# Search units of the second head group moved into the Q, K, V projection stage

## The chip, the cores and the metric

The kernel is one program on one core of a Trainium2 chip. The time is the device time of one execution in microseconds; an execution is compared as the median of several runs of the same program.

## The reference, cut to what matters

Four layers follow one another on a sequence of 1024 tokens with 512 features, each with a residual and a layer normalisation behind it: a selective scan, a gated feed-forward layer, causal attention, and a feed-forward layer with 4-bit weights. The change touches the attention alone:

```python
q, k, v = (proj(wq), proj(wk), proj(wv))          # 32 heads of 16
q = _apply_rope(q, sin, cos)
k = _apply_rope(k, sin, cos)
scores = jnp.einsum('bnth,bnsh->bnts', q, k) * (1.0 / math.sqrt(h))
scores = jnp.where(causal, scores, -jnp.inf)
attn = jax.nn.softmax(scores, axis=-1)
out = jnp.einsum('bnts,bnsh->bnth', attn, v)
```

## The kernel before

PE is TensorE, DVE is VectorE, ACT is ScalarE, POOL is GpSimd, SP is the engine that issues the DMAs. The eight PSUM banks are the array `ps`; `arena` is one large SBUF array in which the buffers are views. All waits between engines are written out by hand as semaphores.

**Attention in head groups.** The 32 heads are worked on in 8 groups of 4 (`g` = 0 to 7), and each group in two halves of 512 query tokens (`half`). The softmax needs the largest score of every query row before the exponentials. So the scores are made twice: a **search** makes them with tokens on the partitions and DVE takes the row maximum (`reduce_max`, L1277); later the **keys** step makes them transposed (L705), with the negated maximum riding along as an extra row of the query operand, ACT takes the exponential (L954), POOL cuts the causal corner (L1054), and **values** multiplies by V (L721).

A **search unit** (`max_units`) is one query tile of 128 tokens against up to 512 keys for one head, or for two heads where two fit in a PSUM bank (L657); on the diagonal two small matmuls add the causal mask (L661). A group has 40 units: tile 0 and tile 1 have 2 each, tiles 2 and 3 have 4 each, tiles 4 and 5 have 6 each, tiles 6 and 7 have 8 each.

**The ring.** Every unit is written to a PSUM bank of a ring and may be written only after DVE has read the unit that was there before (`ring_slot`). In the projection stage the ring has two banks, in the attention it has three:

```python
elif n >= EARLY + RING:
    pe.wait_ge(ring_read, n - RING + 1)
elif n >= 2:
    pe.wait_ge(ring_read, n - 1)
```

**From maximum to key row.** When the units of a half are reduced, DVE negates the maxima (`negate`, L1296, L1298), PE turns them into rows (`turn_maxima`, L692), DVE copies the rows out (L1304), SP puts them with four small DMAs into the query operand (L411), and the first keys step of that group and half waits for these DMAs (`m_rows`).

**The Q, K, V projection stage.** For each of the eight token tiles `t`, PE makes the projections Q, K and V (`project`, L573, 12 matmuls each; `w` = 0, 1, 2), and behind the Q and the K projection it turns the tile before with 16 transposes (`turn_stack`, L634). DVE applies the rotary tables after Q and after K (`rope`, L1266 to L1268) and copies the turned keys (`keep_keys`, L1272). ACT and POOL split the result into two halves of the precision (L924, L1031, L1035). Search units of group 0 for tiles 0 to 5 (24 units, `EARLY_UNITS`) are already made here, those of tile `t - 2` in the iteration `t`, in up to three **places**, one behind each projection, two units per place:

```python
for n in early_units(t, w):
    pe.wait_ge(k_kept, t - 1)
    search(0, *EARLY_UNITS[n], n)
```

DVE reads the units of place 0 between the two `rope` calls, and those of the places 1 and 2 after the second `rope` and `keep_keys`:

```python
rope(0, t)
for n in early_units(t, 0):
    maxima(*EARLY_UNITS[n], n)
rope(1, t)
if t:
    keep_keys(t - 1)
for n in early_units(t, 1) + early_units(t, 2):
    maxima(*EARLY_UNITS[n], n)
```

**The order of the attention.** `attention_order` writes one list (`ORDER`) of all remaining units, negations, turns, keys and values steps, and all engines follow it. The "side" list (searches, negations, turns) and the "main" list (keys and values) are merged by a small model of the engines: at each point it takes what could start first. Early units are left out of the side list, so with fewer of them the whole merge comes out differently. The searches run about one group ahead of the keys.

Of the kernel before, what the change touches and what calls it, by code (L numbers as in the profile page):

```python
# [9 lines left out]
TT = T // P  # L10
# [12 lines left out]
GH = 4  # L23
# [34 lines left out]
def build(nc, x_fm, a_log, d_skip, xw, dtw, wg0, wu0, wd0, wq, wk, wv, wo,  # L58
          w1_q, w1_s, w1_z, ident, fold, mask, cos, sin, shifts, out):
    f32, f16, bf16, i32, u8 = mybir.dt.float32, mybir.dt.float16, mybir.dt.bfloat16, mybir.dt.int32, mybir.dt.uint8  # L60
    ALU = mybir.AluOpType
# [5 lines left out]
    with ctx:  # L67
# [83 lines left out]
        o_tok = view(32, TT * D, f32).rearrange("p (i d) -> p i d", i=TT)  # L151
        o_raw = view(188, T, f32)
        m_row = view(192, T, f16)
        m_a = view(199, TT * GH, f32).rearrange("p (i a) -> p i a", i=TT)
        m_b = view(199.25, 4 * GH, f32).rearrange("p (i a) -> p i a", i=4)
        m_neg = [view(199.5 + h / 8, 4 * GH, f16).rearrange("p (i a) -> p i a", i=4) for h in range(2)]
        r_den = view(199.75, 4 * GH, f32).rearrange("p (i a) -> p i a", i=4)
        oh = view(96, DC * T, f16).rearrange("p (c t) -> p c t", c=DC)
# [37 lines left out]
            return units  # L196
        SEARCH = [max_units(half) for half in range(2)]
        EARLY_TILES = TT - 2
        EARLY_UNITS = [(half, k) for half in range(2) for k, unit in enumerate(SEARCH[half]) if unit[0] < EARLY_TILES]
        EARLY = len(EARLY_UNITS)  # L200

        def early_units(t, place):

            units = [n for n, (half, k) in enumerate(EARLY_UNITS) if SEARCH[half][k][0] == t - 2]
            return units[2 * place:2 * place + 2]

        def maxima_slot(half, k):

            i, key, _, heads = SEARCH[half][k]
            dst = m_b[:, i - 4, :] if key else m_a[:, i, :]  # L210
            r, b = heads[0]
            return dst[:, b:GH:2] if len(heads) == 2 else dst[:, 2 * r + b:2 * r + b + 1]

# [21 lines left out]
        def attention_order():  # L235
# [9 lines left out]
            for g in range(NG):  # L245
                for half in range(2):
                    for k in range(len(SEARCH[half])):
                        if k == TURN_AFTER:
                            side, turn = side + turn, []
                        if g or (half, k) not in EARLY_UNITS:  # L250
                            side.append(("search", g, half, k))
                    side.append(("negate", g, half))
                    if g == 0 and half == 0:
                        side.append(("turn", g, half))
                    else:
                        turn = [("turn", g, half)]
# [64 lines left out]
        def ring_bank(n):  # L321
            return n % 2 if n < EARLY else (n - EARLY) % RING
# [119 lines left out]
        def _(pe):  # L442
# [222 lines left out]
            for t in range(1, TT):  # L665

                for w, signal in ((0, q_proj), (1, k_proj), (2, v_proj)):
                    if w:
                        pe.wait_ge(roped, 2 * t - 2 + w)
                    elif t >= 2:  # L670
                        pe.wait_ge(v_kept, t - 1)
                    project(w, xh, xl, t, qkv_bank(t, w), signal)
                    if w == 0 and t >= 2:
                        pe.wait_ge(k_kept, t - 1)
                    if w == 1:
                        pe.wait_ge(q_kept, t)
                    if w < 2:
                        turn_stack(w, t - 1)
                    for n in early_units(t, w):
                        pe.wait_ge(k_kept, t - 1)  # L680
                        search(0, *EARLY_UNITS[n], n)
            pe.wait_ge(k_kept, TT - 1)
            turn_stack(0, TT - 1)
            pe.wait_ge(q_kept, TT)
# [391 lines left out]
        def _(dve):  # L1076
# [194 lines left out]
                dve.wait_ge(k_turned, t + 1)  # L1271
                nc.vector.tensor_copy(k_st[:, :, ds(t * P, P)], banks(6, 2).bitcast(f16).rearrange("p (r t) -> p r t", r=NP)).then_inc(k_kept, 1)  # L1272

            def maxima(half, k, n):
                _, _, w, heads = SEARCH[half][k]
                dve.wait_ge(ring_full, n + 1)
                nc.vector.reduce_max(maxima_slot(half, k), ps[:, ring_bank(n), 0:len(heads) * w].rearrange("p (a w) -> p a w", a=len(heads)),  # L1277
                                     AX).then_inc(ring_read, 1)

            for t in range(TT):  # L1280
# [11 lines left out]
            def negate(g, half):  # L1292
                last = RING_AT.get(("search", g, half, len(SEARCH[half]) - 1), EARLY - 1)
                dve.wait_ge(ring_read, last + 1)
                if half:
                    nc.vector.tensor_tensor(m_a[:, 4:TT, :], m_a[:, 4:TT, :], m_b[:], ALU.max).then_inc(m_joined, 1)  # L1296
                    dve.wait_ge(m_joined, g + 1)
                nc.vector.tensor_scalar(m_neg[half][:], m_a[:, 4 * half:4 * half + 4, :], -1.0, None, ALU.mult).then_inc(m_negated, 1)  # L1298

            def keep_rows(g, half, n):  # L1300
                dve.wait_ge(ring_full, n + 1)
# [26 lines left out]

            for kind, g, half, *at in ORDER:
                if kind == "search":  # L1330
                    maxima(half, *at, RING_AT[kind, g, half, *at])
                elif kind == "negate":
                    negate(g, half)
                elif kind == "turn":
                    keep_rows(g, half, RING_AT[kind, g, half])
                elif kind == "out":
                    if g == NG - 1 and half == 1:
                        dve.wait_ge(ld_shift, 16)
                        nibbles(0, 0, 1)
                        dve.wait_ge(st_full, EXP_TO[-1])  # L1340
                        unscaled(0)
                        nibbles(1, 1, 1)
                    divide(g, half, RING_AT[kind, g, half])
# [105 lines left out]
```

## Time and profile before

| what | value |
|---|---|
| median of 3 runs | 942.63 us (940.75 to 944.0) |
| profiled execution, its own time | 939.31 us |
| span of its trace | 937.6 us |
| PE busy | 822.3 us (88%) |
| DVE busy | 670.3 us (71%) |
| ACT busy | 398.6 us (43%) |
| POOL busy | 297.3 us (32%) |
| projection stage, main part | 411.7 to 488.0 us |
| attention | 493.6 to about 723 us |

Busy time is the share in which an engine executes instructions; it is an average over stages with different limits, so the stages are read one by one. The span begins at the first instruction and ends at the last; the 1.7 us to the execution's own time lie around it. The first search reduction starts at 428.0 us and the last at 698.9 us.

### The profile page before, as it was taken

The numbers are of one execution on the slowest core, as the hardware profiler recorded it, in microseconds if no ns is written. First come the engines' busy times: TensorE is split into PE (matmuls) and PEld (weight loads), VectorE is DVE, ScalarE is ACT, GpSimd is POOL, SyncE is SP. The second block draws the span as 40 slices with busy tenths as digits, with TensorE's granted clock in tenths as the row PEclk, the third lists the DMA queues.
The fourth block names the chain that finished last, engine by engine and source line by source line (L and its number), as shares of the span: only waits on it lengthen the run. The fifth ranks groups of instructions, "written<-read, shape, count | busy, mean of one in ns | idle before, by whom it ended". The sixth has DMA issues, their size and how long they took to land.

```text
span 937.6 us, 19520 instructions
## 1 busy us (share of the span) xinstructions
PE 822.3 (88%) x8096; PEld 386.3 (41%) x8096; DVE 670.3 (71%) x932; ACT 398.6 (43%) x455; POOL 297.3 (32%) x211
## 2 busy tenths in 40 slices
PE   5556877776799999999998999999996999999997
PEld 1323333332544444445553334444431544444443
DVE  2899999997755334454567899999984878886344
ACT  3623646443253331144342667666675433333100
POOL 0356798988201001035441111122213223222000
PEclk9577899989799999999996899999999999999999
DMA  6700000001620000000000000000003203430011
GB/s 231 309 2 1 3 3 2 3 3 35 211 91 18 0 0 1 1 1 1 1 1 1 2 1 2 2 2 2 2 2 120 99 2 111 142 129 0 1 40 50
DMA packets 20222, 38.23 MB, mean 41 GB/s; under 512 B 6801, under 2 KB 10641, under 8 KB 20146
## 3 DMA queue, kind: packets, MB, share of 16 engines
q1 hardware_dynamic: 20146, 37.12, 11.4%
q8 instruction: 59, 0.97, 0.4%
q14 instruction: 17, 0.14, 0.0%
HBM read 34.89 MB, written 2.16 MB: 40 GB/s over the span
## 4 chain that ended last, share of the span: by engine, by line
PE 62%; DVE 11%; POOL 2%; ACT 2%; issue 1%; SPq 1%; DMA 1%; DVEq 0%; POOLq 0%; ACTq 0%
PE ps L770 12%; PE ps L595 10%; PE ps L573 8%; PE ps L797 6%; DVE arena L1277 6%; PE ps L721 5%; PE ps L619 5%; PE ps L657 5%; PE ps L705 3%; POOL arena L1007 2%; PE ps L634 2%; PE ps L661 1%; PE ps L730 1%; PE ps L462 1%; PE ps L542 1%
## 5 line engine op out<-in xcount | busy, mean ns | idle before, releaser
L1277 DVE TENSOR_REDUCE arena<-ps 128x1 f32<-128x512 f32 (+3 forms) x320 | 183.7, 629 | 20.7 <-PE ps L661 14.7
L1007 POOL TENSOR_TENSOR arena<-arena 128x1024 f32<-128x1024 f32 x64 | 157.0, 2476 | 72.9 <-DVE arena L1133 72.6
L954 ACT ACTIVATE arena<-ps 128x1024 f32<-128x1024 f32 (+2 forms) x160 | 144.1, 941 | 77.9 <-PE ps L705 77.7
L1133 DVE TENSOR_TENSOR_SCAN arena<-arena,ps 128x1024 f32<-128x1024 f32 x64 | 142.9, 2272 | 6.2 <-ACT arena L853 3.8
L770 PE MATMUL ps<-arena 128*128 128x512 f16 x528 | 114.3, 379 | 1.6 <-DVE arena L1212 1.6
L853 ACT ACTIVATE arena<-arena,negA 128x1024 f32<-128x1024 f32 x64 | 73.2, 1148 | 85.6 <-DVE arena L1133 83.4
L1054 POOL TENSOR_SCALAR_AFFINE_SELECT arena<-arena 128x512 f32<-128x512 f32 x64 | 42.5, 664 | 185.5 <-ACT arena L954 185.5
L492 PE MATMUL ps<-arena 64*128 64x64 f16 x3072 | 63.1, 200 | 43.0 <-DVE arena L1133 39.0
L595 PE MATMUL ps<-arena 128*128 128x512 f16 x448 | 98.6, 383 | 1.6 <-DVE arena L1212 1.6
L657 PE MATMUL ps<-arena 64*128 64x512 f16 (+3 forms) x384 | 97.6, 342 | 0.7 <-DVE arena L1277 0.5
L492 PEld LDWEIGHTS ps<-arena 64*128 64x128 f16 x3072 | 55.3, 101 | 102.3 <-DVE arena L1133 83.6
L462 PE MATMUL ps<-arena,ident_sb 64*64 64x512 f32 x512 | 78.3, 687 | 15.4 <-DVE arena L1142 12.3
L573 PE MATMUL ps<-arena 128*128 128x512 f16 x384 | 86.9, 379 | 3.0 <-DVE arena L1212 1.6
L721 PE MATMUL ps<-arena 128*32 128x512 f32 (+3 forms) x768 | 83.8, 509 | 1.9 <-POOL arena L1054 1.9
L705 PE MATMUL ps<-arena 64*128 64x512 f16 (+3 forms) x384 | 77.5, 338 | 4.3 <-DMA arena<-arena 2.3
L770 PEld LDWEIGHTS ps<-arena 128*128 128x128 f16 x528 | 51.6, 98 | 63.6 <-DVE arena L1212 1.8
L595 PEld LDWEIGHTS ps<-arena 128*128 (+1 forms) x448 | 44.2, 99 | 55.4 <-issue 2.1
L657 PEld LDWEIGHTS ps<-arena 64*128 64x128 f16 x384 | 29.2, 94 | 82.1 <-DVE arena L1277 69.8
L797 PE MATMUL ps<-arena 128*128 128x512 f16 x264 | 57.1, 379 | 0.0
L573 PEld LDWEIGHTS ps<-arena 128*128 128x128 f16 x384 | 36.4, 98 | 45.0 <-DVE arena L1186 1.8
L661 PE MATMUL ps<-mask_b,picks_b 64*128 64x128 bf16 x512 | 52.4, 219 | 0.0
L619 PE MATMUL ps<-arena 128*128 128x512 f16 x224 | 49.3, 379 | 0.0
(121 smaller groups left out, 940.9 us busy)
## 6 DMA issues: line engine op xcount, KB each, us to landing
arena<-in_w_q_dram SPq DMA_DIRECT2D x11, 768.0 KB, 4.2
arena<-c_rows SPq DMA_DIRECT2D x16, 512.0 KB, 9.7
arena<-in_w_s_dram SPq DMA_DIRECT2D x11, 384.0 KB, 4.5
arena<-in_x_fm_dram SPq DMA_DIRECT2D x4, 512.0 KB, 5.4
out_dram<-arena SPq DMA_DIRECT2D x8, 256.0 KB, 2.0
arena<-in_wg_dram SPq DMA_DIRECT2D x1, 1792.0 KB, 9.5
arena<-in_wu_dram SPq DMA_DIRECT2D x1, 1792.0 KB, 7.4
arena<-in_wd_dram SPq DMA_DIRECT2D x1, 1792.0 KB, 12.3
```

The source lines that it names most:

```text
L492: last = nc.tensor.matmul(ps[:, 2 * (i % 2) + r, q * SUB:(q + 1) * SUB], dtx_tok[c % 2][rows, s, q, :], diag[n][rows, e, q, :], start=(k = ...
L573: last = nc.tensor.matmul(banks(bank, 1), part[:, c, ds(t * P, P)], wsp[:, w, s, c, :], start=(c == 0 and part is src_h and s == 0), stop= ...
L595: last = nc.tensor.matmul(banks(bank + h, 1), w[:, c, ds(m * P, P)], part[:, c, h * HALF:(h + 1) * HALF], start=(c == 0 and part is xh), s ...
L657: last = nc.tensor.matmul(dst, q_st[rows, 2 * g + r, i * P:(i + 1) * P], k_st[rows, 2 * g + r, key:key + w], start=True, stop=not diag)
L705: last = nc.tensor.matmul(ps[:, 3 + 2 * (e % 2) + b, at * (hi - lo):(at + 1) * (hi - lo)], k_st[rows, 2 * g + r, j * P:(j + 1) * P], q_st[ ...
L721: last = nc.tensor.matmul(ps[32 * a:32 * a + 32, 7, lo - HALF * half:HALF], v_ring[g % 2][:, j, a, :], p_t[n % 4][:, a, 0:hi - lo], start= ...
L770: last = nc.tensor.matmul(banks(bank + h, 1), gu[u][:, s, w * DC + c, :], part[:, c, h * HALF:(h + 1) * HALF], start=(c == 0 and s == 0 an ...
L797: last = nc.tensor.matmul(banks(u, 1), part[:, m, ds(t * P, P)], wd1[:, s, m, :], start=(m == 0 and part is h1h and s == 0), stop=(m == M1 ...
L954: nc.scalar.activation(dst, src, ACT.Exp, scale=float(HD) ** -0.5).then_inc(exp_done, 1)
L1007: nc.gpsimd.tensor_tensor(hC[i % 4][:], hst[i % 3][:], c_all[:, n, :], ALU.mult).then_inc(hc_done, 1)
L1133: nc.vector.tensor_tensor_scan(hst[i % 3][:], dA[i % 3][:], banks(2 * (i % 2), 2), 0.0, ALU.mult, ALU.add).then_inc(scan_done, 1)
L1277: nc.vector.reduce_max(maxima_slot(half, k), ps[:, ring_bank(n), 0:len(heads) * w].rearrange("p (a w) -> p a w", a=len(heads)), AX).then_i ...
```

## The change

The search units of groups 0 and 1 for the tiles 0 to 5 are now both made in the projection stage: 48 units in place of 24, four per place in place of two, group 0 and group 1 alternating. The buffers for the maxima (`m_a`, `m_b`) are doubled, one set per parity of the group. The ring in the projection stage keeps its two banks. The side list of the attention order loses the 24 units of group 1.

```diff
@@ -151,8 +151,8 @@
-        m_a = view(199, TT * GH, f32).rearrange("p (i a) -> p i a", i=TT)
-        m_b = view(199.25, 4 * GH, f32).rearrange("p (i a) -> p i a", i=4)
+        m_a = [view(199 + u / 8, TT * GH, f32).rearrange("p (i a) -> p i a", i=TT) for u in range(2)]
+        m_b = [view(199.25 + u / 16, 4 * GH, f32).rearrange("p (i a) -> p i a", i=4) for u in range(2)]
@@ -196,18 +196,19 @@
-        EARLY_UNITS = [(half, k) for half in range(2) for k, unit in enumerate(SEARCH[half]) if unit[0] < EARLY_TILES]
+        EARLY_GROUPS = 2
+        EARLY_UNITS = [(g, half, k) for half in range(2) for k, unit in enumerate(SEARCH[half]) if unit[0] < EARLY_TILES for g in range(EARLY_GROUPS)]
...
-            units = [n for n, (half, k) in enumerate(EARLY_UNITS) if SEARCH[half][k][0] == t - 2]
-            return units[2 * place:2 * place + 2]
+            units = [n for n, (_, half, k) in enumerate(EARLY_UNITS) if SEARCH[half][k][0] == t - 2]
+            return units[2 * EARLY_GROUPS * place:2 * EARLY_GROUPS * (place + 1)]
@@ -247,7 +248,7 @@
-                        if g or (half, k) not in EARLY_UNITS:
+                        if (g, half, k) not in EARLY_UNITS:
@@ -678,7 +679,7 @@
-                        search(0, *EARLY_UNITS[n], n)
+                        search(*EARLY_UNITS[n], n)
@@ -1293,9 +1294,9 @@
-                    nc.vector.tensor_tensor(m_a[:, 4:TT, :], m_a[:, 4:TT, :], m_b[:], ALU.max).then_inc(m_joined, 1)
+                    nc.vector.tensor_tensor(m_a[g % 2][:, 4:TT, :], m_a[g % 2][:, 4:TT, :], m_b[g % 2][:], ALU.max).then_inc(m_joined, 1)
```

The remaining lines of the diff pass the group's number through `maxima_slot` and `maxima`. Since one line is added, lines of the changed kernel have a number one higher (L657 is L658 there).

On PE in the projection stage, iteration t = 5, from the transposes behind the K projection to the V projection (place 1; L634 are the transposes, L657 and L661 a search unit, L573 a projection), before:

```order
L634 MATMUL ps<-ident_h,arena 128x128 x15
L657 MATMUL ps<-arena 128x512 [waits ring_read,k_kept]
L661 MATMUL ps<-mask_b,picks_b 128x128 x2
L657 MATMUL ps<-arena 128x512 [waits ring_read,k_kept]
L661 MATMUL ps<-mask_b,picks_b 128x128 x2
L573 MATMUL ps<-arena 128x512 [waits roped]
```

and in the changed kernel:

```order
L635 MATMUL ps<-ident_h,arena 128x128 x15
L658 MATMUL ps<-arena 128x512 [waits ring_read,k_kept]
L662 MATMUL ps<-mask_b,picks_b 128x128 x2
L658 MATMUL ps<-arena 128x512 [waits ring_read,k_kept]
L662 MATMUL ps<-mask_b,picks_b 128x128 x2
L658 MATMUL ps<-arena 128x512 [waits ring_read,k_kept]
L662 MATMUL ps<-mask_b,picks_b 128x128 x2
L658 MATMUL ps<-arena 128x512 [waits ring_read,k_kept]
L662 MATMUL ps<-mask_b,picks_b 128x128 x2
L574 MATMUL ps<-arena 128x512 [waits roped]
```

Two units more stand ahead of the V projection, and each unit waits for the reading of the unit two before it.

On DVE in the same stretch, from the second `rope` of t = 5 (L1266 to L1268) over `keep_keys` (L1272) to the reductions (L1277), before:

```order
L1266 TENSOR_TENSOR arena<-ps,cos_sb 128x512 [waits stack_low,k_proj]
L1267 TENSOR_TENSOR arena<-ps,sin_sb 128x32x8
L1268 TENSOR_TENSOR arena<-ps,sin_sb 128x32x8
L1272 COPY arena<-ps 128x16x128 [waits k_turned]
L1277 TENSOR_REDUCE arena<-ps 128x1 [waits ring_full] x2
```

and in the changed kernel:

```order
L1267 TENSOR_TENSOR arena<-ps,cos_sb 128x512 [waits stack_low,k_proj]
L1268 TENSOR_TENSOR arena<-ps,sin_sb 128x32x8
L1269 TENSOR_TENSOR arena<-ps,sin_sb 128x32x8
L1273 COPY arena<-ps 128x16x128 [waits k_turned]
L1278 TENSOR_REDUCE arena<-ps 128x1 [waits ring_full] x4
```

The reductions still stand behind `rope` and `keep_keys`, and there are four of them.

On DVE at the start of the attention, from the last searches of group 0 (L1277) over the negation (L1296, L1298) and the copy of the rows (L1304), before:

```order
L1277 TENSOR_REDUCE arena<-ps 128x1 [waits ring_full] x16
L1296 TENSOR_TENSOR arena<-arena 128x16 [waits ring_read]
L1298 TENSOR_SCALAR arena<-arena 128x16 [waits m_joined]
L1277 TENSOR_REDUCE arena<-ps 128x2 [waits ring_full] x2
L1304 COPY arena<-ps 4x512 [waits ring_full]
L1277 TENSOR_REDUCE arena<-ps 128x2 [waits ring_full] x2
L1277 TENSOR_REDUCE arena<-ps 128x1 [waits ring_full] x8
```

and in the changed kernel:

```order
L1278 TENSOR_REDUCE arena<-ps 128x1 [waits ring_full] x16
L1297 TENSOR_TENSOR arena<-arena 128x16 [waits ring_read]
L1299 TENSOR_SCALAR arena<-arena 128x16 [waits m_joined]
L1305 COPY arena<-ps 4x512 [waits ring_full]
L1299 TENSOR_SCALAR arena<-arena 128x16 [waits ring_read]
L1305 COPY arena<-ps 4x512 [waits m_rows0,ring_full]
L1278 TENSOR_REDUCE arena<-ps 128x1 [waits ring_full] x13
```

The rows of group 0, half 1 and of group 1, half 0 now follow each other directly, and the search units of group 1 for the tiles 0 to 5 are gone from here.

## Rows read from the trace of the kernel before

**Rows 1.** Busy time by stretch: start and end, length, engines busy, PEclk.

```profile
411.70:488.00 76.30, 76.30 (x569) 41.59 (x570) 41.24 (x78) 35.13 (x32) 37.99 (x32) 1.00 0.01 1
493.64:525.00 31.36, 29.08 (x203) 11.00 (x204) 23.50 (x46) 12.42 (x14) 2.54 (x4) 0.67 0.01 1
525.00:552.16 27.16, 26.55 (x276) 11.02 (x273) 25.07 (x50) 18.77 (x22) 5.63 (x9) 1.00 0.01 2
660.80:687.96 27.16, 26.56 (x276) 11.02 (x273) 25.06 (x50) 18.77 (x22) 5.63 (x9) 1.00 0.01 2
687.96:698.30 10.34, 10.34 (x103) 3.63 (x98) 9.75 (x17) 7.24 (x9) 2.54 (x4) 1.00 0.00 0
```

The five busy times are those of PE, PEld (weight loads), DVE, ACT and POOL; behind them stand the granted clock of PE, the share of the DMA engines and GB/s.

**Rows 2.** Chain of waits, 440 to 492 us, shares by line.

```profile
by line: PE ps L573 69.1%; PE ps L634 19.4%; PE ps L657 6.0%; ACT arena L915 3.6%; PE ps L661 2.2%; issue 0.1%
```

**Rows 3.** Timeline of t = 5: start, length, engine, line, operation, [idle before].

```profile
458.59 0.40 PE L657 MATMUL ps<-arena 64*128 64x512 f16 x2
459.03 2.76 PE L573 MATMUL ps<-arena 128*128 128x512 f16 x12
459.12 1.29 DVE L1277 TENSOR_REDUCE arena<-ps 128x1 f32<-128x512 f32 x2
462.62 0.40 PE L657 MATMUL ps<-arena 64*128 64x512 f16 x2
463.06 5.35 PE L573 MATMUL ps<-arena 128*128 128x512 f16 x24
463.10 1.21 DVE L1272 COPY arena<-ps 128x2048 f16<-128x2048 f16 x1
464.23 1.28 DVE L1277 TENSOR_REDUCE arena<-ps 128x1 f32<-128x512 f32 x2
```

**Rows 4.** Timeline, reductions and projections at the places of other iterations.

```profile
427.96 0.76 DVE L1277 TENSOR_REDUCE arena<-ps 128x2 f32<-128x256 f32 x2
448.52 1.02 DVE L1277 TENSOR_REDUCE arena<-ps 128x1 f32<-128x384 f32 x2
452.41 5.35 PE L573 MATMUL ps<-arena 128*128 128x512 f16 x24
453.63 1.01 DVE L1277 TENSOR_REDUCE arena<-ps 128x1 f32<-128x384 f32 x2
476.71 0.76 DVE L1277 TENSOR_REDUCE arena<-ps 128x2 f32<-128x256 f32 x2 [0.67 <-PE ps L661]
476.73 2.76 PE L573 MATMUL ps<-arena 128*128 128x512 f16 x12
487.90 1.29 DVE L1277 TENSOR_REDUCE arena<-ps 128x2 f32<-128x512 f32 x2 [0.78 <-PE ps L661]
```

**Rows 5.** Timeline of the attention: the ring runs full; below, one reduction alone.

```profile
508.19 3.75 DVE L1277 TENSOR_REDUCE arena<-ps 128x2 f32<-128x512 f32 x7
508.93 0.09 PEld L657 LDWEIGHTS ps<-arena 64*128 64x128 f16 x1 [0.47 <-DVE arena L1277]
509.53 0.09 PEld L657 LDWEIGHTS ps<-arena 64*128 64x128 f16 x1 [0.33 <-DVE arena L1277]
...
592.43 0.69 DVE L1277 TENSOR_REDUCE arena<-ps 128x2 f32<-128x512 f32 x1
```

**Rows 6.** Timeline at the end of the attention, where no search is left.

```profile
704.50 0.39 PE L705 MATMUL ps<-arena 64*128 64x512 f16 x2 [1.12 <-DMA arena<-arena]
704.99 2.86 ACT L954 ACTIVATE arena<-ps 128x1024 f32<-128x1024 f32 x3 [1.69 <-PE ps L705]
710.45 7.89 ACT L954 ACTIVATE arena<-ps 128x1024 f32<-128x1024 f32 x9 [0.28 <-PE ps L705]
```

**Rows 7.** Busy time by stretch, where the clock of PE falls or holds.

```profile
180.00:192.00 12.00, 9.44 (x292) 4.79 (x284) 12.00 (x7) 5.74 (x6) 11.33 (x6) 1.00 0.02 4
488.00:494.00 6.00, 2.44 (x39) 2.01 (x38) 2.50 (x4) 1.86 (x1) 1.57 (x3) 1.00 0.00 0
494.00:504.00 10.00, 9.41 (x48) 3.12 (x46) 8.43 (x15) 4.41 (x5) 1.27 (x2) 0.51 0.01 0
```

More of the change, by code:

```diff
@@ L198, in build, with maxima_slot @@
         EARLY_TILES = TT - 2
-        EARLY_UNITS = [(half, k) for half in range(2) for k, unit in enumerate(SEARCH[half]) if unit[0] < EARLY_TILES]
+        EARLY_GROUPS = 2
+        EARLY_UNITS = [(g, half, k) for half in range(2) for k, unit in enumerate(SEARCH[half]) if unit[0] < EARLY_TILES for g in range(EARLY_GROUPS)]
         EARLY = len(EARLY_UNITS)
         def early_units(t, place):
-            units = [n for n, (half, k) in enumerate(EARLY_UNITS) if SEARCH[half][k][0] == t - 2]
-            return units[2 * place:2 * place + 2]
-        def maxima_slot(half, k):
+            units = [n for n, (_, half, k) in enumerate(EARLY_UNITS) if SEARCH[half][k][0] == t - 2]
+            return units[2 * EARLY_GROUPS * place:2 * EARLY_GROUPS * (place + 1)]
+        def maxima_slot(g, half, k):
             i, key, _, heads = SEARCH[half][k]
-            dst = m_b[:, i - 4, :] if key else m_a[:, i, :]
+            dst = m_b[g % 2][:, i - 4, :] if key else m_a[g % 2][:, i, :]
             r, b = heads[0]
@@ L1272, in keep_keys, with maxima @@
                 nc.vector.tensor_copy(k_st[:, :, ds(t * P, P)], banks(6, 2).bitcast(f16).rearrange("p (r t) -> p r t", r=NP)).then_inc(k_kept, 1)
-            def maxima(half, k, n):
+            def maxima(g, half, k, n):
                 _, _, w, heads = SEARCH[half][k]
                 dve.wait_ge(ring_full, n + 1)
-                nc.vector.reduce_max(maxima_slot(half, k), ps[:, ring_bank(n), 0:len(heads) * w].rearrange("p (a w) -> p a w", a=len(heads)),
+                nc.vector.reduce_max(maxima_slot(g, half, k), ps[:, ring_bank(n), 0:len(heads) * w].rearrange("p (a w) -> p a w", a=len(heads)),
                                      AX).then_inc(ring_read, 1)
@@ L1295, in negate @@
                 if half:
-                    nc.vector.tensor_tensor(m_a[:, 4:TT, :], m_a[:, 4:TT, :], m_b[:], ALU.max).then_inc(m_joined, 1)
+                    nc.vector.tensor_tensor(m_a[g % 2][:, 4:TT, :], m_a[g % 2][:, 4:TT, :], m_b[g % 2][:], ALU.max).then_inc(m_joined, 1)
                     dve.wait_ge(m_joined, g + 1)
-                nc.vector.tensor_scalar(m_neg[half][:], m_a[:, 4 * half:4 * half + 4, :], -1.0, None, ALU.mult).then_inc(m_negated, 1)
+                nc.vector.tensor_scalar(m_neg[half][:], m_a[g % 2][:, 4 * half:4 * half + 4, :], -1.0, None, ALU.mult).then_inc(m_negated, 1)
             def keep_rows(g, half, n):
@@ L1330, in _ @@
                 if kind == "search":
-                    maxima(half, *at, RING_AT[kind, g, half, *at])
+                    maxima(g, half, *at, RING_AT[kind, g, half, *at])
                 elif kind == "negate":
```

## The prediction

> **What bounds the kernel now.** I read the busy time by stretch first. In the projection stage PE is busy in all of its 76.30 us, DVE in 41.24 [rows 1]: to the reader this says that DVE has 35 us to spare, and that whatever delays PE here delays the kernel. The chain of waits agrees: from 440 to 492 us nearly all of it is PE, projections, transposes and searches [rows 2], with no wait for DVE in it. In the attention six equal periods of 27.16 us follow each other, one per head group; the first and the last of them are shown, with PE busy 26.55, DVE 25.07 and ACT 18.77 us [rows 1]. There both PE and DVE are nearly full. So the change takes reductions from where DVE is short and puts them where it has time. The question is whether PE can hand them over there without standing still. For that I read the timeline of one iteration [rows 3], then the same places of the others [rows 4].
>
> **Part 1, two more units at each place.** The units stand in the order t = 2 and 3: place 0 alone; t = 4 and 5: places 0 and 1; t = 6 and 7: places 0, 1 and 2. That is 12 places: six of place 0, four of place 1, two of place 2. Before, the two units of a place found both banks of the ring free. Now the third must wait until DVE has read the first, and the fourth until it has read the second; PE takes its queue in order, so the projection behind them waits too. All ACT and POOL work of the iteration is fed by that projection and is late by the same amount.
>
> The projection before started at P; DVE started its reductions at D. Now it starts at D + R + 0.05 + 0.35. R is the length of two reductions. 0.05 is the hand-over from DVE to PE: a read that starts at 508.19 ends at 508.88, since one read of this size takes 0.69, and PE loads the next unit's weights at 508.93 [rows 5]. 0.35 is the fourth unit's own time on PE: a pair takes 0.44 (458.59 to 459.03) [rows 3], and one unit alone lies between half of this and all of it. The delay is thus (D - P) + R + 0.40.
>
> - Place 0: D - P is 459.12 - 459.03 = 0.09 [rows 3], and I take it for all six. R is 0.76 for tile 0, 1.29 for tile 1 (same size as the last row of the group), 1.02 for tile 2, 1.29 for tiles 3, 4 and 5 [rows 3, 4]: 6.94. Delay 6 x 0.49 + 6.94 = 9.9 us.
> - Place 1: here DVE has `rope` and `keep_keys` ahead of the reductions, which it starts long after PE has gone on: 464.23 - 463.06 = 1.17 and 453.63 - 452.41 = 1.22 [rows 3, 4]; the waits of `rope` are on the projection, so this distance moves along with PE. With 1.2: 4 x (1.2 + 0.40) + 1.01 + 3 x 1.28 = 11.3 us.
> - Place 2: D - P is 0 (476.71 against 476.73), R is 0.76 and 1.29 [rows 4]: 2 x 0.40 + 2.05 = 2.9 us.
>
> Sum: 24.1 us later at the end of the stage. Bounds: if PE never stood still, only the work of 12 pairs would be added, 12 x 0.44 = 5.3 us; if each unit alone took a full pair's time, 12 x 0.09 more, 25.2 us. I take 24.1, because the row of the attention's ring shows just this behaviour: with the ring full, PE's loads wait 0.47 and 0.33 us for DVE and follow it at its pace [rows 5]. Nothing covers it: PE is the busy engine. DVE's 13.9 us of added reductions (2 pairs at 0.76, 2 at 1.02, 8 at 1.29 [rows 3, 4]) fit into its idle time.
>
> **Part 2, the attention without 24 units.** The start: until the negation of group 0, half 1, the order is unchanged. Then two reductions fall away between negation and row copy, which brings the DMAs of the rows forward by some 0.1 us; the four DMAs of group 1, half 0 stand behind them in SP's queue, and nobody waits for those until much later. The first keys step of half 1 still waits for its rows, and the four units left in front of it don't fill that time as the eight before did. From there to step j = 3 of that half there are 14 units beside the same main steps, before and now. So this stretch, the one of low clock (0.67 from 493.64 to 525.00 [rows 1]), costs the same: 0. Of the 24 units, 5 are lost in the DMA wait, and 19 are the searches' new lead over the keys.
>
> The six periods have the same 40 units and the same 18 main steps in another merge: 0 is my value. DVE could at best save its idle time, 2.09 us each, 12.5 us in all; a worse merge could cost, and I allow 0.5 us each, 3 us, by the waits of rows 5.
>
> The end: before, the last 17 searches run from 687.96 to 698.30, 10.34 us beside main work in which ACT is busy 7.24 us [rows 1]. Now main work is alone there. With no searches left, ACT does 9 exponentials in 7.89 us without a gap [rows 6], so this stretch becomes ACT's, 7.9 us with its gaps: a gain of 2.4. The last rows now arrive long before the first keys step of the last half, which waited 1.12 us on PE and 1.69 on ACT [rows 6]: a gain of 1.4, between the two. Together the attention gives back **3.8 us**. Its bounds: +3 us (the worse merge and nothing at the end), and -13.9 us, if DVE were the bound throughout and each reduction came back in full.
>
> By busy time PE would bound the periods (26.55 of 27.16). The Trainium skill, Perfetto Trace Analysis, Identifying the Most-Contended Engine, says that matmul busy time is no measure of PE's load, and points to weight loads instead; these are 11.02 us of a period [rows 1], and DVE with 25.07 is then the contended engine. By that rule the attention would give back the whole 13.9 us; this is rival 1.
>
> **Sum:** 939.31 + 24.1 - 3.8 = 959.6 us for the profiled execution. It lay 3.3 us below the median of its runs (942.63), so the median becomes 942.63 + 20.3 = **962.9 us**.
>
> **The rivals.**
> 1. *DVE bounds the attention throughout.* For it: 25.07 of 27.16 us. Against it: the periods hold main work that ACT and PE must still do when the searches are gone, and the stretch at the end shows 7.24 us of it in 10.34. Gain 13.9 in place of 3.8: 942.63 + 24.1 - 13.9 = 952.8 us.
> 2. *The clock of PE falls in the projection stage.* It fell to half, the 1.2 GHz level, at 494, after 6 us in which PE was busy 2.44 us [rows 7]. In place 1 PE will be nearly idle for some 3 us, beside 5.4 us of dense projections. Against it: in the scan stage PE is busy 9.44 of 12 us at full clock [rows 7], and the projection stage will be busier than that (76.3 of about 100 us plus the new units). If it falls in each of the four iterations with place 1 and half of their 8 us of projections takes twice as long: +16, 979 us. The Trainium skill, TensorE: Matmul & The Clock Gate, PE-mode transpose, says that transposes don't count as activity for this clock; by that rule the 0.9 us of transposes ahead of each wait would belong to the quiet stretch, which favours this rival. No row here decides it.
> 3. *Faster.* The longer lead of the searches lets the six periods shrink to DVE's own time, 12.5 us, and the 24 units come back in full, 13.9: 942.63 + 24.1 - 26.4 = 940.3 us; a little less waiting at the places takes it below. It decides in the attention: the periods would have to fall from 27.16 below 25.5 us, 24.1 less 13.9 over six of them. Against it: no stretch of the attention shows DVE without gaps, and every period has keys steps that wait for ACT.
> 4. *The ring doesn't hold PE up* (5.3 us in place of 24.1), for instance if DVE reached the units earlier: 942.63 + 5.3 - 3.8 = 944.1 us. Against it: the row order on DVE puts `rope` and `keep_keys` ahead.
>
> **How the numbers follow.** Forecast 0.68, rival 1 0.13, rival 2 0.12, rival 3 0.04, rival 4 0.03. The forecast's own range: waits 22 to 26 us, attention -8 to +3, so 957 to 971. The range from 950 to 972 takes in rival 1 and leaves out rivals 2 to 4, 2 in 10 at most. About 0.3%, 2.8 us, is what a measurement of this kernel can tell from no change. Rivals 3 and 4 lie about there and share their 0.07 between faster and same; all else is slower: 0.04, 0.03, 0.93.
>
> **What the profile would show.** Right: the stage from the first rope to the last transposes is some 24 us longer; PE waits for DVE's reductions at 12 places, about 0.8 and 0.3 us at place 0 and 1.9 and 0.3 at place 1; its clock stays 1.00 there; six periods of about 27.2 us; the last search about 11 us earlier, measured from the attention's start, than before; no DMA wait at the last half. Wrong: no waits for DVE in the projection stage, periods clearly shorter or longer than 27, or a clock of 0.50 before the attention.

## The result, and the profile after

The changed kernel takes **963.0 us** (median of 4 runs, 962.63 to 964.47), the kernel before 942.09 us in the same comparison: ratio 1.0223, 95% interval 1.0202 to 1.0245. It is slower by 20.9 us. Its profiled execution took 962.79 us with a span of 961.1, next to its median; that of before (939.31) lay 2.8 us below its kernel's median, so the two traces differ by 23.5 us. Below, the traces tell where time went, and medians tell how much.

The busy time by stretch answers to [rows 1]: the projection stage up to the last pair of transposes, the attention's start, and one full period. Columns: start and end, length, then PE, PEld, DVE, ACT and POOL busy, the granted clock, the DMA share and GB/s.

```profile
412.13:518.91 106.78, 94.87 (x649) 50.02 (x649) 55.45 (x102) 35.10 (x32) 39.55 (x34) 0.95 0.00 1
525.00:555.63 30.63, 26.16 (x191) 9.97 (x191) 22.93 (x48) 13.54 (x16) 2.54 (x4) 0.72 0.01 2
608.86:635.70 26.84, 26.60 (x276) 11.09 (x272) 25.00 (x50) 18.67 (x23) 5.63 (x9) 1.00 0.01 2
```

The same stretch of the stage took 76.28 us before. PE, which had no idle time there, now stands still for 12 us, and its clock is no longer 1.00. DVE's 14.2 us of added work fit in easily, as it has 51 us to spare. The period of the attention is 0.32 us shorter.

The chain of waits between 440 and 525 us, shares by line, answers to [rows 2]:

```profile
by line: PE ps L574 49.7%; DVE arena L1278 10.5%; PE ps L658 7.9%; DVE arena L1273 6.8%; DVE arena L1267 6.5%; PE ps L635 4.5%; PE ps L662 3.4%; DVE arena L1268 3.1%; DVE arena L1269 3.1%; issue 2.5%; ACT arena L916 2.2%
```

Before, nearly all of it was PE. Now 30% is DVE: its reductions (L1278), but also `rope` (L1267 to L1269) and `keep_keys` (L1273), which stand ahead of the reductions of place 1. The ring has made DVE's whole queue part of PE's path.

The timelines of PE and DVE at t = 5 answer to [rows 3]. Columns: start, length, engine, line, operation, and in brackets the idle time before it and what ended it. Place 0 comes first, place 1 below:

```profile
468.81 2.65 DVE L1278 TENSOR_REDUCE arena<-ps 128x1 f32<-128x512 f32 x4
469.64 0.37 PE L658 MATMUL ps<-arena 64*128 64x512 f16 x1 [0.55 <-DVE arena L1278]
470.24 0.37 PE L658 MATMUL ps<-arena 64*128 64x512 f16 x1
470.66 2.76 PE L574 MATMUL ps<-arena 128*128 128x512 f16 x12
...
474.59 0.38 PE L658 MATMUL ps<-arena 64*128 64x512 f16 x1
474.73 1.22 DVE L1273 COPY arena<-ps 128x2048 f16<-128x2048 f16 x1
475.86 2.75 DVE L1278 TENSOR_REDUCE arena<-ps 128x1 f32<-128x512 f32 x4
476.69 0.37 PE L658 MATMUL ps<-arena 64*128 64x512 f16 x1 [1.61 <-DVE arena L1278]
477.28 0.39 PE L658 MATMUL ps<-arena 64*128 64x512 f16 x1
```

The brackets put the third unit's wait at 0.55 us at place 0 and 1.61 at place 1; the fourth follows 0.6 us behind it at the pace of DVE's reading. The brackets leave out what the small matmuls of the second unit still overlap: by the starts, the third unit comes 0.8 us (place 0) and 1.9 us (place 1) later than the 0.22 us at which units follow each other where nothing holds them, as the prediction had it.

That is the part foreseen. What comes behind it was only a rival: the projections behind place 1 of t = 4, 5 and 6 are slower than the 5.35 and 2.76 us that the same counts took before (columns as above; below, the busy time and clock in three stretches of theirs):

```profile
460.40 7.04 PE L574 MATMUL ps<-arena 128*128 128x512 f16 x24
477.81 6.87 PE L574 MATMUL ps<-arena 128*128 128x512 f16 x24
494.67 4.39 PE L574 MATMUL ps<-arena 128*128 128x512 f16 x12
```

```profile
460.00:464.00 4.00, 3.96 (x13) 1.55 (x13) 1.02 (x2) 0.25 (x1) 1.44 (x2) 0.57 0.00 0
478.00:480.00 2.00, 2.00 (x6) 0.68 (x5) 0.61 (x1) 0.00 (x0) 0.46 (x1) 0.50 0.03 8
494.00:498.00 4.00, 3.78 (x10) 1.29 (x10) 1.47 (x3) 0.30 (x1) 1.49 (x2) 0.57 0.00 0
```

PE is dense again there, but at half clock, the 1.2 GHz level, and only back at 1.00 behind some 3 us of projections. It is the fall that [rows 7] show at 494 us of before, where PE had been busy 2.44 of 6 us between the stages, now inside the stage. Each fall costs about 1.6 us: 1.69 + 1.52 + 1.63 = 4.8. The fall at the end of the stage comes sooner too: at 494 us of before it lies behind the last 16 transposes, in the change ahead of them, and they take 1.89 us in place of 1.07.

In the attention, ACT's copies of the outputs (two per group, one per half) mark how far the main work is. Of before, those that end the first, the seventh and the eighth group:

```profile
536.73 0.59 ACT L940 COPY arena<-ps 128x512 f32<-128x512 f32 x1
...
699.68 0.59 ACT L940 COPY arena<-ps 128x512 f32<-128x512 f32 x1
...
721.54 0.58 ACT L940 COPY arena<-ps 128x512 f32<-128x512 f32 x1 [3.19 <-PE ps L721]
```

and of after, those that end the first, second, sixth, seventh and eighth group:

```profile
566.86 0.59 ACT L941 COPY arena<-ps 128x512 f32<-128x512 f32 x1
...
593.36 0.59 ACT L941 COPY arena<-ps 128x512 f32<-128x512 f32 x1
...
700.71 0.59 ACT L941 COPY arena<-ps 128x512 f32<-128x512 f32 x1
...
724.12 0.61 ACT L941 COPY arena<-ps 128x512 f32<-128x512 f32 x1
...
744.63 0.58 ACT L941 COPY arena<-ps 128x512 f32<-128x512 f32 x1 [3.42 <-PE ps L722]
```

The attention is taken from the first negation (493.25 before, 525.00 after) to the last reciprocal of the denominators (725.12, 747.99): 231.87 us before, 222.99 after, 8.9 less. Piece by piece: up to the first group's end 43.48 and 41.86 us (-1.6); then six periods, before 162.95 together, after 26.50, four times 26.84 and a last one of 23.41, together 157.26 (-5.7, of which -3.75 in the last, in which the searches end 7.9 us before the group does); the eighth group 21.86 and 20.51 (-1.35: its wait for the rows of [rows 6] is gone); and 0.2 behind it.

So the traces add up as follows: +0.4 us ahead of the stage, +31.3 in it (from its first projection to the negation), -8.9 in the attention, +0.6 behind it: 23.5 us.

### The profile page after: what moved, and what is told of

The parts are those of the page before. It is cut to its first block, busy times and chain, and to the rows that moved or that the text cites. A ratio compares the mean times of both kernels' runs of the same rounds, so it can differ in the third digit from the quotient of the medians.

```text
span 961.1 us, 19544 instructions
## 1 busy us (share of the span) xinstructions
PE 835.2 (87%) x8096; PEld 392.9 (41%) x8096; DVE 670.4 (70%) x932; ACT 397.8 (41%) x455; POOL 297.2 (31%) x211
## 4 chain that ended last, share of the span: by engine, by line
PE 61%; DVE 12%; issue 2%; ACT 2%; POOL 2%; SPq 0%; DMA 0%; DVEq 0%; ACTq 0%; POOLq 0%
PE ps L771 12%; PE ps L596 10%; PE ps L574 8%; PE ps L798 6%; PE ps L722 6%; DVE arena L1278 5%; PE ps L620 5%; PE ps L658 5%; PE ps L706 3%; PE ps L662 2%; POOL arena L1008 2%; PE ps L731 1%; ACT arena L955 1%; PE ps L463 1%; PE ps L543 1%
## 5 line engine op out<-in xcount | busy, mean ns | idle before, releaser
L1278 DVE TENSOR_REDUCE arena<-ps 128x1 f32<-128x512 f32 (+3 forms) x320 | 183.3, 629 | 22.6 <-PE ps L662 19.5
L771 PE MATMUL ps<-arena 128*128 128x512 f16 x528 | 114.3, 379 | 1.6 <-DVE arena L1213 1.6
L658 PE MATMUL ps<-arena 64*128 64x512 f16 (+3 forms) x384 | 103.7, 341 | 13.5 <-DVE arena L1278 12.4
L596 PE MATMUL ps<-arena 128*128 128x512 f16 x448 | 98.6, 383 | 1.6 <-DVE arena L1213 1.6
L493 PEld LDWEIGHTS ps<-arena 64*128 64x128 f16 x3072 | 55.6, 101 | 102.4 <-DVE arena L1134 83.5
L574 PE MATMUL ps<-arena 128*128 128x512 f16 x384 | 91.7, 394 | 3.1 <-DVE arena L1213 1.6
L706 PE MATMUL ps<-arena 64*128 64x512 f16 (+3 forms) x384 | 76.1, 338 | 4.6 <-ACT arena L955 2.5
L658 PEld LDWEIGHTS ps<-arena 64*128 64x128 f16 x384 | 31.2, 94 | 87.8 <-DVE arena L1278 53.1
L798 PE MATMUL ps<-arena 128*128 128x512 f16 x264 | 57.1, 379 | 0.0
L662 PE MATMUL ps<-mask_b,picks_b 64*128 64x128 bf16 x512 | 57.0, 220 | 0.0
L620 PE MATMUL ps<-arena 128*128 128x512 f16 x224 | 49.3, 379 | 0.0
```

What stands on the lines that cost most here:

```text
L493: last = nc.tensor.matmul(ps[:, 2 * (i % 2) + r, q * SUB:(q + 1) * SUB], dtx_tok[c % 2][rows, s, q, :], diag[n][rows, e, q, :], start=(k = ...
L574: last = nc.tensor.matmul(banks(bank, 1), part[:, c, ds(t * P, P)], wsp[:, w, s, c, :], start=(c == 0 and part is src_h and s == 0), stop= ...
L596: last = nc.tensor.matmul(banks(bank + h, 1), w[:, c, ds(m * P, P)], part[:, c, h * HALF:(h + 1) * HALF], start=(c == 0 and part is xh), s ...
L658: last = nc.tensor.matmul(dst, q_st[rows, 2 * g + r, i * P:(i + 1) * P], k_st[rows, 2 * g + r, key:key + w], start=True, stop=not diag)
L706: last = nc.tensor.matmul(ps[:, 3 + 2 * (e % 2) + b, at * (hi - lo):(at + 1) * (hi - lo)], k_st[rows, 2 * g + r, j * P:(j + 1) * P], q_st[ ...
L771: last = nc.tensor.matmul(banks(bank + h, 1), gu[u][:, s, w * DC + c, :], part[:, c, h * HALF:(h + 1) * HALF], start=(c == 0 and s == 0 an ...
```

## The experiments

Eight further kernels were run. Two stretches of each profiled execution serve as a scale: the **stage**, from the projections that begin at some 412 us (411.70 in [rows 1]) to the negation of group 0, half 0; and the **attention**, from there to the last reciprocal.

| kernel | stage, us | attention, us | median, us |
|---|---|---|---|
| before | 81.55 | 231.87 | 942.09 |
| the change | 112.87 | 222.99 | 963.00 |
| e1 stage alone | 112.84 | 230.73 | 970.25 |
| e2 attention alone | 81.62 | 222.52 | 931.61 |
| e3 place 1 sooner | 102.64 | 224.03 | 953.37 |
| e4 six places | 89.31 | 222.59 | 939.11 |
| e5 pair order | 112.87 | 223.03 | 963.71 |
| e6 filled, projection | 107.12 | 222.46 | 956.93 |
| e7 filled, transposes | 107.11 | 222.42 | 957.04 |
| e8 units put back | 81.55 | 234.89 | 944.45 |

The stage repeats to 0.1 us where its order is the same. What scatters between executions is the start of the attention, with its low clock (41.3 to 42.9 us to the first group's end in the kernels with the order of the change, e8 apart; 41.5 and 43.5 with that of before), and the time at which the stage begins (411.2 to 414.5 us).

### e1 and e2: each half of the change by itself

e1 makes group 1's early units in both stages; e2 makes them in neither (their places in the buffers of the maxima are set to zero).

```diff
-                        if (g, half, k) not in EARLY_UNITS:
+                        if g or (g, half, k) not in EARLY_UNITS:
```

```diff
+        EARLY_UNITS = [(0, half, k) for half in range(2) for k, unit in enumerate(SEARCH[half]) if unit[0] < EARLY_TILES]
+        LEFT_OUT = [(g, half, k) for _, half, k in EARLY_UNITS for g in range(EARLY_GROUPS)]
...
-                        if (g, half, k) not in EARLY_UNITS:
+                        if (g, half, k) not in LEFT_OUT:
...
```

> The projection stage of the change, with the attention's order of before: the 24 units of group 1 are made in the projection stage and once more in the attention. Theory A (the cost lies in the projection stage alone: waits of PE for DVE at 12 places plus a slower clock behind some of them, +31 us from the first projection to the negation of group 0, half 0; nothing else is touched): the attention takes 231.9 us as before, total 942.1 + 31 = 973 us (971 to 976). Theory B (the ring does not hold PE up, and the time is lost elsewhere): the stage costs only the work of 12 pairs, +5.3 us, total 947 us. Theory C (the attention of the change was merely shifted, and gave nothing back): total equal to the change's, 963 us.

> The attention of the change with the projection stage of before. The 24 units of group 1 for the tiles 0 to 5 are made nowhere; their places in the buffers of the maxima hold zero, so this part of the computation is left out. Theory A (the traces of the two kernels read stretch by stretch: start -2.0, six periods -3.65, end -3.2): 942.1 - 8.9 = 933.2 us (931.5 to 935), with periods of 26.84 us. The forecast's own terms (start 0, periods 0, end -3.8): 938.3 us, with periods of 27.16. Theory B (DVE bounds the attention, each reduction comes back in full, 13.9 us): 928.2 us.

e1 took 970.25 us (ratio 1.0295, 1.0271 to 1.0318), e2 931.61 (0.9887, 0.9863 to 0.9911). Both come out as theory A has them, e1 0.75 us below its range. The cost is all in the stage: e1 has the change's stage to 0.03 us and, with the order of before, nearly the attention of before, with periods of 27.15 to 27.16 us behind a second one of 28.02. And the attention gives back its part beside either stage: e2's is 9.35 us shorter than before's, the change's 7.7 us shorter than e1's.

The medians say the same less sharply. By them the stage costs 28.2 us (e1 over before) or 31.4 (the change over e2), and the attention gives back 10.4 (e2 under before) or 7.3 (the change under e1). So some 3 us depend on which stage and which order stand together, or are scatter of the medians: the runs don't part the two. About half of it shows in the traces, in the attention's first two groups. The forecast's term of 3.8 us would have given e2 938.3, a DVE-bound attention 928.2; neither is near.

### e3: place 1 read sooner

```diff
                 rope(1, t)
+                for n in early_units(t, 1):
+                    maxima(*EARLY_UNITS[n], n)
                 if t:
                     keep_keys(t - 1)
-                for n in early_units(t, 1) + early_units(t, 2):
+                for n in early_units(t, 2):
```

> The change, with one move on DVE: the four reductions of place 1 stand ahead of keep_keys instead of behind it, so that D - P at place 1 falls from 1.2 to about 0.1 us. Theory A (PE's wait there is the formula's, and its length is also what makes the clock fall behind place 1 in three iterations): four places by 1.1 us, -4.5, and the clock stays 1.00, -4.8 us more: 963.0 - 9.3 = 953.7 us (952 to 956). Theory B (the clock falls whatever the length of this wait): -4.5 alone, 958.5 us. Theory C (keep_keys, now 1.2 us later or more, holds up PE's next unit of the next iteration or the turned stack): no gain, 961 to 964 us.

953.37 us (1.0126, 1.0102 to 1.015): theory A's number. Place 1 of t = 5 on PE in this kernel:

```profile
471.90 0.37 PE L658 MATMUL ps<-arena 64*128 64x512 f16 x1 [0.55 <-DVE arena L1278]
472.49 0.37 PE L658 MATMUL ps<-arena 64*128 64x512 f16 x1
472.91 5.35 PE L574 MATMUL ps<-arena 128*128 128x512 f16 x24
```

The wait is place 0's 0.55 us in place of 1.61, and the projections behind it take 5.35 us, as before the change. The stage is 10.2 us shorter: 4.8 by the clock, 0.8 by the very last transposes (they now run at full clock, 1.07 in place of 1.89 us), the remaining 4.6 by the waits, 1.15 at each of the four places. `keep_keys`, 2.2 us or more later, holds nobody up. So D - P, the distance between PE's and DVE's arrival, was the right quantity.

### e5: is it the order of the units?

```diff
+        EARLY_UNITS.sort(key=lambda unit: (unit[1], unit[2] // 2, unit[0], unit[2]))
```

> The change with its 48 early units in another order: within each tile a pair of group 0, then the pair of group 1, instead of the two groups alternating; places, waits and counts stay. Theory A (the cost comes from two units more per place, whichever they are): 963 us, within 1.5. Theory B (the alternation of the groups costs, since neighbouring units read different operands): over 2 us faster.

963.71 us (1.0238, 1.0208 to 1.0268), and the stage the same to the hundredth. Which units share a place makes no difference; this also clears e4, which sorts them so.

### e6 and e7: what makes the clock fall

Both fill the wait ahead of the third unit of place 1, at t = 4 to 7, with work that has no use, six matmuls in e6 and 20 transposes in e7 (shown).

```diff
+            def filler(t):
+                pe.wait_ge(roped, 2 * t)
+                for r in range(20):
+                    nc.tensor.transpose(banks(qkv_bank(t, 2), 1).bitcast(f16)[:, (r % 8) * P:(r % 8 + 1) * P], ident_h[:], ident_h[:])
...
-                    for n in early_units(t, w):
+                    for k, n in enumerate(early_units(t, w)):
                         pe.wait_ge(k_kept, t - 1)
+                        if w == 1 and k == 2:
+                            filler(t)
```

> The change, with six matmuls of the V projection made one time more ahead of the third unit of place 1 (t = 4 to 7; the bank is the one that the V projection starts anew right afterwards, so the result stays). They take 6 matmuls of the 2.76 us for 12, 1.3 us, and lie within a wait of 1.58 to 1.84 us. Theory A (the clock falls behind place 1 since PE stands still there): the clock stays 1.00 up to the end of the stage, the 4.8 us of slower projections vanish, the waits stay: 963.0 - 4.8 = 958 us (957 to 960). Theory B (the fall has another cause, such as the search units' half-height operands): the clock falls as before, 963 us. Theory C (the added matmuls delay the third unit): slower than 963.

> The same with 20 transposes of the identity (16 take 1.06 us, so 20 take 1.3) in place of the six matmuls. Theory A (any work of PE in this wait holds the clock): 958 us and a clock of 1.00, as with the matmuls. Theory B (transposes are too sparse an activity): the clock falls at the same three places, 963 us. The Trainium skill, TensorE: Matmul & The Clock Gate, PE-mode transpose, says that transposes don't count as activity for the clock, which is theory B.

e6 took 956.93 us (1.0157, 1.0128 to 1.0187), e7 957.04 (1.0157, 1.0127 to 1.0187). Adding work made the kernel 6 us faster. Around place 1 of t = 5 in e7, the added transposes, the third unit and the projections behind the place:

```profile
475.69 1.29 PE L668 MATMUL ps<-ident_h 128*128 128x128 f16 x20
477.29 0.39 PE L658 MATMUL ps<-arena 64*128 64x512 f16 x1 [0.30 <-DVE arena L1285]
...
478.39 5.35 PE L574 MATMUL ps<-arena 128*128 128x512 f16 x24
```

and the busy time and clock behind it:

```profile
478.00:482.00 4.00, 4.00 (x20) 1.84 (x21) 1.19 (x2) 0.60 (x1) 1.15 (x1) 1.00 0.00 0
```

The third unit still starts behind DVE's reading; only most of PE's idle time is gone, and with it the fall: the clock is 1.00 up to the last transposes, and the stage is 5.75 us shorter in both (4.8 for the three falls, 0.8 for the last transposes). PE's standing still is thus what brings the clock down at these three places, not the shape of the searches; the fourth place shows, in the last section, that it doesn't do so every time. Theory B for transposes falls: here they hold the clock as well as matmuls. The Trainium skill, TensorE: Matmul & The Clock Gate, PE-mode transpose, has it that the full clock doesn't engage for transposes, since they don't count as busy time in the same way. These runs contradict it as far as holding the full clock goes: 1.00 and 5.35 us behind 20 transposes, as behind six matmuls. Whether transposes alone would bring the clock up, no run here shows.

### e4: the same work without the queue

```diff
+        EARLY_UNITS.sort(key=lambda unit: (unit[1], unit[2] // 2, unit[0], unit[2]))
         EARLY = len(EARLY_UNITS)
+        PLACES = {4: (0, 1), 8: (0, 1, 2, 4), 12: (0, 1, 2, 3, 4, 5)}
...
-            return units[2 * EARLY_GROUPS * place:2 * EARLY_GROUPS * (place + 1)]
+            at = PLACES.get(len(units), ())
+            return units[2 * at.index(place):2 * at.index(place) + 2] if place in at else []
...
-            def project(w, src_h, src_l, t, bank, signal):
+            def project(w, src_h, src_l, t, bank, signal, between=None, after=2):
                 for c in range(DC):
+                    if c == after and between is not None:
+                        between()
...
+                    project(w, xh, xl, t, qkv_bank(t, w), signal, lambda: early(*((t - 1, 5), (t, 1), (t, 3))[w]), (2, 2, 3)[w])
...
-                for n in early_units(t, 0):
+                for n in early_units(t, 0) + early_units(t, 1):
...
```

> All the work of the change, but never more than two units one behind the other in the projection stage: six places of one pair each (behind the first transposes, in the middle of the K projection, behind the second transposes, in the middle of the V projection, behind it, and in the middle of the next Q projection). Theory A (the change costs what it does since the third and fourth unit of a place wait for DVE; the work alone is 24 pairs in place of 12, +5.3 us; the clock stays 1.00; the attention gives back 8.9): 942.1 + 5.3 - 8.9 = 938.5 us, up to 941 with 0.4 us of waits at some places; faster than both kernels. Theory B (DVE, which has rope and keep_keys ahead of the pairs in the middle, still holds PE up at two places of each iteration by about 1 us): 945 to 950 us. Theory C (the interruptions in the middle of a projection delay rope and so everything behind it): over 950 us.

939.11 us (median of 12 runs, ratio 0.9976, 0.9963 to 0.9989): 24 us less than the change with the same operations, and faster than before by 0.24%, which the interval just tells from no change. On PE, first the pair behind the second transposes of t = 5, the V projection and the pair behind it; then, in t = 6, the pair behind the first transposes and the K projection, cut in two by the next pair:

```profile
465.32 0.40 PE L663 MATMUL ps<-arena 64*128 64x512 f16 x2
...
465.76 2.76 PE L579 MATMUL ps<-arena 128*128 128x512 f16 x12
468.46 0.40 PE L663 MATMUL ps<-arena 64*128 64x512 f16 x2
...
472.49 0.39 PE L663 MATMUL ps<-arena 64*128 64x512 f16 x2
472.81 1.47 PE L579 MATMUL ps<-arena 128*128 128x512 f16 x6
474.22 0.55 PE L663 MATMUL ps<-arena 64*128 64x512 f16 x2
474.70 1.47 PE L579 MATMUL ps<-arena 128*128 128x512 f16 x6
```

No bracket stands behind any of these rows: the units find both banks read. Over the whole stage the clock is 1.00 and PE busy 86.61 of 89.31 us:

```profile
411.26:500.57 89.31, 86.61 (x680) 46.60 (x680) 57.33 (x104) 36.98 (x33) 39.59 (x34) 1.00 0.00 1
```

The stage costs 7.8 us more than before. The lengths in these rows don't add up to that, as each overlaps the start of the next; from start to start they do. Eleven of the twelve added pairs take 6.4 us, two of them, in the V projections of t = 6 and 7, held up by DVE and 0.90 us long in place of 0.48. The twelfth costs nothing, since it falls into PE's wait for ACT ahead of the last transposes. The other 1.3 us are 0.12 at each of the eleven interruptions: the K projection of t = 6 takes 1.41 and 1.31 us to what follows each half, in place of 2.60 for a whole one. The forecast's 5.3 us for a ring that never holds PE up left out these interruptions.

That the ring's two banks hold PE up when four units stand in a row is shown by this; whether a third bank in this stage would do as well as the spreading was not tried.

### e8: does the attention gain by less work or by another order?

The projection stage is that of before, and `LEFT_OUT` is that of e2; what is added is

```diff
+        for half, mark in ((0, ("negate", 1, 0)), (1, next(step for step in ORDER if step[:3] == ("search", 1, 1)))):
+            at = ORDER.index(mark)
+            ORDER[at:at] = [("search", 1, *unit[1:]) for unit in LEFT_OUT if unit[:2] == (1, half)]
```

> The projection stage of before and the attention's order of the change, in which the 24 units of group 1 are put back in two lumps of 12, each at the attention's start with no main work beside it: all work of the kernel before is done again in the attention, and only the merge of searches and main work behind the first periods is the changed one. Theory A (the six periods of 26.84 us and the shorter end come from the new merge and from the longer lead of the searches, not from any work that has left the attention): periods 26.84 again, end as in the change; the lumps cost DVE's 13.9 us of reductions, less up to 1 us of idle time that they fill: 931.6 + 13 to 14 = 945 us (943.5 to 946.5). Theory B (a period shortens since the moved units are missing from it): periods of 27.16 again, 947.5 us or more.

944.45 us (1.0022, 1.0003 to 1.004), theory A's range. The joins of the maxima on DVE, two that follow each other, one period apart:

```profile
590.98 0.17 DVE L1301 TENSOR_TENSOR arena<-arena 128x16 f32<-128x16 f32 x1
617.82 0.18 DVE L1301 TENSOR_TENSOR arena<-arena 128x16 f32<-128x16 f32 x1
```

26.84 us, though no work has left the attention. A full period holds the same 40 units and 18 main steps in all these kernels; the 0.32 us are another merge of them. Behind the first group's end e8 has the pieces of the change, the end included (26.51 us, four of 26.83 to 26.85, 23.42, 20.28). So the periods and the end gain by the order and by the searches' longer lead, and not by less work. What the moved work itself is worth lies at the start: made there alone, the 24 units cost 12.4 us of attention (234.89 against e2's 222.52), near the 13.9 us of their reductions. The kernel before, which mixes them with main work, pays about 9 for them. The new order by itself is therefore no gain: with all its work e8's attention is 3.0 us longer than before's.

## Why the prediction came out as it did

The forecast was 962.9 us, the measurement 963.0. That closeness is in part luck, of two kinds. Two terms were too small and have opposite signs. And the profiled execution of before, from which the sum starts, was 2.8 us faster than its kernel's median, that of the change only 0.2: the traces differ by 23.5 us, where the sum had 20.3, the medians by 20.9. Against the profiled execution the sum was 959.6 and the measurement 962.79: the stage came out 7.2 us dearer than forecast, the attention gave back 5.1 us more, and 1.0 us lies ahead of and behind the stretches that the change touches.

**The waits at the 12 places: right.** Forecast +24.1, measured +25.7. Taken from the end of the transposes (or projection) to the next projection, after less before: place 0 10.6 us (forecast 9.9), place 1 11.9 (11.3), place 2 3.2 (2.9). What is missing is small at each place: at t = 5, place 0, the reductions begin at 468.81, R is 1.29, the projection starts at 470.66, so 0.56 us lie behind R where the formula had 0.40. Over the twelve places it is 0.43 to 0.68 us, 0.54 on average. The hand-over to PE is here 0.14 us (the formula had 0.05) and the fourth unit's own time 0.42 (0.35). That nothing would cover the waits was right: e1 shows the stage's whole length in its traced span. D - P as the lever was right: e3.

**The clock in the projection stage: wrong.** "Its clock stays 1.00 there" failed: the cost of the falls was put at nothing and is 4.8 us at three places, and 0.8 more at the last transposes. This was rival 2, as to its cause, and e6 and e7 show that cause directly. Its price of 16 us was not right either: it let half of 8 us of projections run at half clock in four iterations, but the clock is back behind about 3 us, and the fourth iteration had no fall. The argument against it failed: it compared average busy time in the scan stage with that of the whole projection stage. The rule on transposes that it cited from the Trainium skill (TensorE: Matmul & The Clock Gate, PE-mode transpose) spoke for the right side with a reason that e7 refutes.

**The attention, start (0): wrong by 1.6 us, the cause in part open.** The time to the first group's end went from 43.48 to 41.86 us, but e1, with the order of before, has 41.51 there and gives 0.86 us back in the period behind it. Up to the second group's end it is 70.64 us before and 69.53 in e1, 68.36 in the change and 67.91 in e2: the new order is worth 1.2 us behind the stage of the change and 2.7 behind that of before. The rest goes with the stage that stands ahead and with the low clock, and can't be parted further.

**The six periods (0, bounds -12.5 and +3): wrong by 1.9 us** over the first five. The forecast named the merge as the only thing that could change them and took it as neutral; e8 shows that the merge is the cause and the amount of work isn't. The rows of before gave only the bounds for it.

**The end (-3.8): right in kind, too small.** Measured -3.75 in the last period and -1.35 in the eighth group, -5.1 together. The wait for the rows at the last half, put at 1.4, is gone as foreseen. Main work alone without searches, put at 2.4, gave 3.75; the last join of maxima comes 191.2 us after the attention's start in place of 206.4, 15 us sooner and not 11. The searches' longer lead, and not fewer searches, is what e8 shows behind both numbers.

Rival 1 (DVE bounds the attention, -13.9) falls: -8.9 us, and DVE is busy 25.00 of 26.84 us, still not without gaps. The rule on the most-contended engine that stood beside it (the Trainium skill, Perfetto Trace Analysis, Identifying the Most-Contended Engine) pointed at DVE; the period followed the merge instead. Rival 4 fails as a statement on this kernel, but e4 is that rival built: the forecast gave it 944.1, and it takes 939.1. Its stage is 2.5 us dearer than the 5.3 of the rival, and its attention gives back 9.3 us in place of 3.8. That would make 941.1; the other 2 us are scatter between traces and medians (its trace is 1.6 us shorter than that of before, its median 2.9). The total of the change is then

- +25.7 waits, +5.6 clock: +31.3 in the stage,
- -8.9 in the attention,

against +24.1 and -3.8 in the forecast.

## What to carry to other kernels

Moving work into another engine's idle time costs what the hand-over costs at the place where it is put. Two banks serve two units; each further one in a row ties the producer to the consumer's whole queue, here `rope` and `keep_keys` too. So count the units one behind the other against the buffers first, and place them in pairs as far apart as the consumer needs: that alone made 24 us here. Where a wait on PE can't be avoided next to dense work, look at the granted clock behind it as well as at the wait.

## What the runs showed of the hardware that was not expected

**The clock falls on short waits, and not always.** The longest single wait at the places is 1.84 us. The 6 us up to the projection behind place 1 look alike at t = 6 and at t = 7, in the order of the columns above:

```profile
488.70:494.70 6.00, 3.94 (x30) 1.89 (x28) 4.17 (x7) 1.04 (x1) 2.70 (x3) 0.99 0.00 0
507.60:513.60 6.00, 3.94 (x30) 1.91 (x28) 4.13 (x7) 1.04 (x1) 2.66 (x3) 1.00 0.00 0
```

PE is busy 3.94 us in both. Behind the first the clock fell to half (4.39 us for 12 matmuls, shown above), behind the second it didn't:

```profile
513.60 2.76 PE L574 MATMUL ps<-arena 128*128 128x512 f16 x12
```

What parts them stays open. The profiled executions of e1 and e5 fell at the same three places and not at the fourth, though e1's stage began 0.6 us later than the change's, so it is not chance alone.

**Work without use can save time.** 20 transposes in each of four waits of 1.58 to 1.84 us gave back 6.0 us of 963 (e7). It is a remedy only where the wait has to stay; without the wait (e4) the kernel is another 18 us faster.
